# Second feed-forward layer as one block: expert tiles gather and send their own rows, the shared part on both sides of the expert loop

## The reference, cut to what matters

```python
xt = layernorm(x).reshape(-1, 256)                 # 2048 tokens
scores = softmax(xt @ gate_w.T)                    # 15 experts
topk_w, topk_idx = top_k(scores, 3)
topk_w = topk_w / (sum(topk_w) + 1e-20)
comb = zeros((T, 15)).at[arange(T)[:, None], topk_idx].add(topk_w)
h = einsum('td,efd->etf', xt, fc1_w) + fc1_b       # 512 wide per expert
a = gelu(h[..., 256:]) * h[..., :256] * geglu_mult
yexp = einsum('etf,edf->etd', a, fc2_w) + fc2_b
y = einsum('etd,te->td', yexp, comb)
hs = xt @ s_fc1_w.T + s_fc1_b                      # shared part, 2 x 512 wide
ys = (gelu(hs[..., 512:]) * hs[..., :512] * s_mult) @ s_fc2_w.T + s_fc2_b
x = x + y + ys
```

## Time and profile before

| | |
|---|---|
| time, median of 3 | 1479.79 us (1479.38 to 1481.75) |
| time of the profiled execution | 1479.18 us |
| its span | 1477.4 us |
| busy: TensorE, VectorE, ScalarE, GpSimd | 80%, 50%, 35%, 27% |
| mean granted TensorE clock | 0.863 |
| HBM traffic | 91 GB/s over the span |

### The profile page before, as it was taken

One profiled execution on the slowest core, in us unless ns is written; L12 is line 12 of the kernel. 1 busy time (PEld: TensorE's weight loads), 2 busy tenths in 40 slices (PEclk: granted clock), 3 DMA queues, 4 the chain that ended last, 5 costly groups with the idle time before them and its releaser, 6 DMA issues. The chain is left out here.

```text
span 1477.4 us, 20683 instructions
## 1 busy us (share of the span) xinstructions
PE 1175.2 (80%) x6778; PEld 768.4 (52%) x6779; DVE 732.5 (50%) x1364; ACT 521.5 (35%) x1084; POOL 399.5 (27%) x482
## 2 busy tenths in 40 slices
PE   4798993699999999944698989997539989999900
PEld 2323442699999999932243534443325455555500
DVE  5576622355665556453776676751421124444423
ACT  1285550344543345300265454644130112222200
POOL 3153456223332223023121120000066001111156
PEclk9698655799999999975699999979759999999955
DMA  3460101322333222034232231200853112222134
GB/s 97 171 264 23 51 27 43 109 93 72 112 122 112 82 70 81 19 111 128 72 112 91 73 102 52 66 1 1 261 184 142 54 47 82 82 82 78 64 103 132
DMA packets 86460, 135.49 MB, mean 92 GB/s; under 512 B 18504, under 2 KB 55468, under 8 KB 86258
## 3 DMA queue, kind: packets, MB, share of 16 engines
q1 hardware_dynamic: 72050, 92.58, 19.6%
q0 software_dynamic: 14336, 41.94, 8.2%
HBM read 86.98 MB, written 47.71 MB: 91 GB/s over the span
## 5 line engine op out<-in xcount | busy, mean ns | idle before, releaser
L1744 DVE TENSOR_REDUCE M<-S 128x2 f32<-128x1024 f32 x128 | 153.9, 1221 | 39.2 <-PE S L1389 35.1
L1651 ACT ACTIVATE PT<-S 128x512 f32<-128x512 f32 x256 | 138.8, 594 | 83.1 <-PE S L1413 81.3
L2110 PE MATMUL H<-W,XST 128*128 x248 | 122.1, 616 | 5.2 <-issue 5.1
L222 POOL TENSOR_TENSOR w12l<-stage,w12h 128x1024 fp32r<-128x1024 f32 x28 | 67.9, 2427 | 202.2 <-ACT w12h L216 202.1
L1197 DVE TENSOR_TENSOR HTm0l<-HFm,HTm0h 128x320 fp32r<-128x320 f32 x128 | 121.7, 951 | 1.0
L1203 DVE TENSOR_TENSOR HFm<-Um,SGm 128x320 f32<-128x320 f32 x128 | 62.4, 487 | 80.9 <-ACT SGm L1166 80.6
L1166 ACT ACTIVATE SGm<-Gm 128x320 f32<-128x320 f32 x128 | 55.9, 437 | 119.0 <-PE Um L1124 118.1
L2088 POOL DMA_DIRECT2D ys<-YS x62 | 33.5, 541 | 233.2 <-DVE YS L2204 233.2
L1137 PE MATMUL Ym<-w3h,HTm0h 128*128 128x256 f32 x320 | 93.3, 292 | 0.0
L909 DVE TENSOR_REDUCE M<-S 128x2 f32<-128x1024 f32 x64 | 77.1, 1222 | 30.4 <-PE S L426 29.9
L1389 PE MATMUL S<-KS,QS 48*128 48x512 f32 x256 | 70.3, 547 | 25.7 <-DVE M L1744 9.5
(11 more groups left out here) (273 smaller groups left out, 2485.0 us busy)
## 6 DMA issues: line engine op xcount, KB each, us to landing
stage<-in_W12T SPq DMA_DIRECT2D x32, 512.0 KB, 6.2
xs<-zeros POOLq DMA_DIRECT2D x25, 512.0 KB, 5.9
stage<-in_W3T SPq DMA_DIRECT2D x16, 512.0 KB, 3.8
XS<-xs SPq DMA_DIRECT2D x62, 128.0 KB, 2.0
ys<-YS POOLq DMA_DIRECT2D x62, 128.0 KB, 2.0
W<-in_fc1T SPq DMA_DIRECT2D x2, 3840.0 KB, 21.8
KS<-scrk SPq DMA_DIRECT2D x96, 64.0 KB, 2.3
QS<-scrq SPq DMA_DIRECT2D x96, 64.0 KB, 2.2
```

The source lines that it names most:

```text
L222: pool.tensor_tensor(ew.part(1, s, c), ew.stage[:, c % STAGES, :], ew.part(0, s, c).bitcast(F32), ALU.subtract).then_inc(ew.low_done, 1)
L1651: act.activation(PT[:, at % SLICES, 2 * hp + j, :], S2[:, j, :], ACT.Exp, scale=HP ** -0.5).then_inc(exp_done, 1)
L1744: dve.tensor_reduce(M[:, n % 3, at:at + 2 * TPB + 1:2 * TPB], out[:, :, :], AX.X, ALU.max).then_inc(S1.done(("max", c)), 1)
L2110: m = pe.matmul(H[:, c % 2, :], XST[:, c % 2, k, :], W1[:, k, bass.ds(e, 1), :], start=(k == 0), stop=(k == KD - 1))
```

## The change

`route1`, `experts1` and `combine` become one block, `ffn1`.

- The slot of every token-expert pair is no longer used to scatter rows. Instead a table says for each slot which pair sits in it: with lo and hi the low 7 bits and the rest of the slot's number, VectorE writes one-hots LO (128x1024) and HI (128x496) for 8 token tiles at a time, GpSimd multiplies HI by the pair's number + 1, and TensorE sums LO transposed by HV into a 128x62 table in PSUM. There are 6 such chunks. Empty slots get a target past the end.
- GpSimd gathers each expert tile's rows from XF in HBM (`fetch`) and scatters its 128 results to yk, ordered by pair (`send`, out-of-range targets are dropped). Fetch j+4 is written ahead of send j on GpSimd's queue. xs1 and its fills go.
- fc2_b is added to each expert tile's result on VectorE, in place of the product with comb; s_fc2_b is added to X by GpSimd.
- The shared part of batches 0 and 1 stays ahead of the expert loop, that of batches 2 and 3 follows it. There, the weighted addition of yk rows (loaded by SP, contiguous) is interleaved on VectorE with the shared part, one token tile after each of its elements.
- Layer 1 stores XF to HBM, and loads and scales the shared weights.

The diff, cut to its core:

```diff
 # layer0
-                (env.xs0, E0 * CAP0, filled0), (env.xs1, TILES1 * P, filled1)) for r in range(0, rows_, ZROWS)]
+                (env.xs0, E0 * CAP0, filled0),) for r in range(0, rows_, ZROWS)]
 # layer1
+                    if t == ends(b) + 6:
+                        sp.wait_ge(xn_done[1], b + 1)
+                        sp.dma_start(env.xf.rearrange("(b t p) d -> b p t d", p=P, t=TPB)[b],
+                                     XF[:, b % 2 * TPB:(b % 2 + 1) * TPB, :]).then_inc(env.xf_stored, 16)
+                if t == 40:
+                    load_shared()
+                if t == 90:
+                    pool.wait_ge(env.shared_loaded, 16 * 6)
+                    for j in range(FFS // P):
+                        ins_ = pool.tensor_scalar(env.s2[:, j, :], env.s2[:, j, :], smul[:, j:j + 1], None, ALU.mult)
 # ffn1, SP
+            for k in range(KF): W2 load
+            for k in range(KD): W1 load
+            sp.wait_ge(decoded, 1)
+            B1 load
+            sp.wait_ge(expert_done, 1)
+            B2 load
+            sp.wait_ge(h_ready, TILES1)
+            for c in range(DEEP):
+                sp.wait_ge(y_sent[c], LAST_YS[c])
+            for t in range(NT):
+                sp.dma_start(YK[:, t, :, :], env.yk.rearrange("(k t p) d -> t p k d", k=K1, p=P)[t]).then_inc(yk_loaded[t], 16)
+            for i, t in enumerate(finished):
+                sp.wait_ge(fin, i + 1)
+                out of tile t
 # ffn1, GpSimd
-                pool.dma_start(ys_tiles[j], YS[:, c, :]).then_inc(y_stored[c], 16)
+            def fetch(j):
+                if j >= DEEP:
+                    pool.wait_ge(xt_ready, j - DEEP + 1)
+                pool.indirect_dma_start(
+                    out=XS[:, j % DEEP, :], out_offset=None, in_=env.xf[:, :],
+                    in_offset=bass.IndirectOffsetOnAxis(ap=env.moves.source[:, j:j + 1], axis=0),
+                ).then_inc(fetched[j % DEEP], 16)
+            def send(j):
+                pool.wait_ge(y_done, j + 1)
+                pool.indirect_dma_start(
+                    out=env.yk[:, :], out_offset=bass.IndirectOffsetOnAxis(ap=env.moves.target[:, j:j + 1], axis=0),
+                    in_=YS[:, j % DEEP, :], in_offset=None, bounds_check=K1 * TOK - 1, oob_is_err=False,
+                ).then_inc(y_sent[j % DEEP], 16)
+            pool.wait_ge(decoded, 1)
+            for j in range(DEEP):
+                fetch(j)
+            for c in range(2, BATCH):
+                shared_bias(c)
+            for j in range(TILES1):
+                if j + DEEP < TILES1:
+                    fetch(j + DEEP)
+                send(j)
 # ffn1, TensorE
+            def place(i):
+                pe.wait_ge(hv_done, i + 1)
+                for t in range(TC):
+                    m = pe.matmul(table, LO[:, i % 2, t, :], HV[:, i % 2, t, :], start=(i == 0 and t == 0),
+                                  stop=(i == CHUNKS - 1 and t == TC - 1))
+                m.then_inc(hot_free, 1)
+            shared_in(0, 0), shared_in(0, 1), rank products, shared_in(0, 2), shared_in(0, 3)
+            place(0)
+            place(1)
+            for q in range(TPB):
+                shared_out(0, q)
+                place(2 + q)
+            shared part of batch 1; the 62 steps; shared part of batches 2 and 3
 # ffn1, VectorE
+            hot(0)
+            hot(1)
+            shared_gate(0, 2)
+            shared_gate(0, 3)
+            for q in range(TPB):
+                hot(2 + q)
+                shared_add(0, q)
+            table to target and source, tiles' experts, weights
-                dve.tensor_copy(YS[:, c % DEEP, :], Y[:, c % 2, 0:D]).then_inc(y_done, 1)
+                dve.tensor_tensor(YS[:, c % DEEP, :], Y[:, c % 2, 0:D], B2[:, bass.ds(e, 1), :].squeeze(1), ALU.add).then_inc(y_done, 1)
```

More of the change, by code:

```diff
@@ L1802, in _, with __init__, ffn1 @@
                         keep_logits(b)
-def combine(nc, env, ex, out):
+class Moves:
+    def __init__(self, sb):
+        self.val = sb("val1", [P, K1, NT])
+        self.source, self.target = sb("source1", [P, TILES1], U32), sb("target1", [P, TILES1], U32)
+FRONT = 2
+HALVES = 2
+CHUNKS = K1 * HALVES
+TC = NT // HALVES
+def ffn1(nc, env, ins, out):
+    JS, KF = FFS // P, FF1 // P
+    FIRST = TPB * FRONT
     with ExitStack() as ctx:
         sb, ps, sem = scope(nc, ctx)
[L1809 to L1829, removed]
@@ L1847, in route1 @@
[L1847 to L1855, removed]
@@ L1856, in route1 @@
[L1856 to L1891, removed]
@@ L2068, in steps @@
                 step(j // DEEP, j % DEEP)
-        xs_tiles = env.xs1[:, :].rearrange("(j p) d -> j p d", p=P)
-        ys_tiles = env.ys1[:, :].rearrange("(j p) d -> j p d", p=P)
+        back = [("in", c, j) if p == 0 else ("out", c, j) for c in range(FRONT, BATCH) for p, j in
+                [(0, j) for j in range(JS)] + [(1, q) for q in range(TPB)]]
+        each = -(-NT // len(back))
+        final, todo = [], list(range(NT))
+        for i, s in enumerate(back):
+            final.append(s)
+            if i >= 1:
+                final += [("rows", t) for t in todo[0:each]]
+                todo = todo[each:]
@@ L2073, in _ @@
+        final += [("rows", t) for t in todo]
+        finished = []
+        for i, s in enumerate(final):
+            for t in range(NT):
+                mine = [("rows", t)] + ([("out", *divmod(t, TPB))] if t >= FIRST else [])
+                if s in mine and all(m in final[0:i + 1] for m in mine):
+                    finished.append(t)
         @block.sync
         def _(sp):
-            def step(r, c):
-                j = r * DEEP + c
-                if not (isinstance(r, int) and j < DEEP):
-                    sp.wait_ge(xt_ready, j - DEEP + 1)
-                sp.dma_start(XS[:, c, :], xs_tiles[j]).then_inc(xs_loaded[c], 16)
@@ L2083, in _, with shared_bias @@
+            sp.wait_ge(sent, 16 * NT)
         @block.gpsimd
         def _(pool):
-            def step(r, c):
-                j = r * DEEP + c
-                pool.wait_ge(y_done, j + 1)
-                pool.dma_start(ys_tiles[j], YS[:, c, :]).then_inc(y_stored[c], 16)
-            steps(pool, step)
-            for c in range(DEEP):
-                pool.wait_ge(y_stored[c], 16 * ((TILES1 - c + DEEP - 1) // DEEP))
+            row = env.s2b[:, :].unsqueeze(1).to_broadcast([P, TPB, D])
+            def shared_bias(c):
+                xb = env.X[:, c * TPB:(c + 1) * TPB, :]
+                pool.tensor_tensor(xb, xb, row, ALU.add).then_inc(biased, 1)
@@ new lines, in shared_out @@
+            def shared_out(c, q):
+                t = c * TPB + q
+                pe.wait_ge(at_done, JS * (c + 1))
+                wait(pe, shared_done, t - 1)
+                for j in range(JS):
+                    m = pe.matmul(pw[:, t % 2, 0:D], AT[:, j, q * P:(q + 1) * P], s2[:, j, :],
+                                  start=(j == 0), stop=(j == JS - 1))
+                m.then_inc(ys_ready, 1)
+            def place(i):
[4 more added lines that the diff above has]
+                m.then_inc(hot_free, 1)
@@ new lines, in _ @@
+            shared_in(0, 0)
+            shared_in(0, 1)
+            pe.wait_ge(run_done, 1)
+            pe.matmul(rk[:, 0:NT, :], env.before[:, :], w.all[:, :, :], start=True, stop=False)
+            pe.matmul(rk[:, 0:NT, :], env.ones[:, :], w.run[:, 0:NT, :], start=False, stop=True)
+            pe.matmul(rk[:, NT, :], env.ones[:, :], w.run[:, NT, :], start=True, stop=True).then_inc(rk_ready, 1)
+            shared_in(0, 2)
+            shared_in(0, 3)
+            place(0)
+            place(1)
@@ L2180, in _ @@
             turn_back(*divmod(TILES1 - 1, DEEP))
+            act.wait_ge(a_done, TILES1)
+            for c in range(FRONT, BATCH):
+                for j in range(JS):
+                    gelu(c, j)
         @block.vector
         def _(dve):
-            dve.wait_ge(env.b1_loaded, 16)
+            link = Link(dve, chain)
+            pick(dve, link, env, w, E1, K1, env.lg[:, :, :], False)
+            dve.nop().then_inc(lg_sub, 1)
+            dve.wait_ge(ex_done, 1)
+            softmax_top(dve, link, env, w, E1, K1, 0.0)
@@ new lines, in _ @@
+            link(dve.tensor_tensor(sq[:, :, :], ntile[:, :].unsqueeze(1).to_broadcast([P, E1, E1]),
+                                   env.earlier[:, :, :], ALU.mult))
+            link(dve.tensor_reduce(base[:, :], sq[:, :, :], AX.X, ALU.add))
+            link(dve.scalar_tensor_tensor(
+                w.lg[:, :, :], base[:, :].unsqueeze(1).to_broadcast([P, NT, E1]), float(P), rk[:, 0:NT, :],
+                ALU.mult, ALU.add))
+            for k in range(K1):
+                link(dve.tensor_tensor(w.tmp[:, :, :], w.lg[:, :, :], w.hot[:, k, :, :], ALU.mult))
+                link(dve.tensor_reduce(w.slot[:, k, :], w.tmp[:, :, :], AX.X, ALU.add))
@@ new lines, in _ @@
+            link(dve.tensor_reduce(w.red[:, :], w.top[:, :, 0:K1], AX.X, ALU.add))
```

(27 more changed lines are left out.)

372 lines of the change are left out of this document (190 added, 182 removed).

## The result

The changed kernel took 1553.05 us (median of 4, 1546.12 to 1558.18) against 1480.77 us before: ratio 1.048, 95% interval 1.0428 to 1.0532. It is slower by 72 us; 43 us faster was forecast. The profiled execution has a span of 1554.6 us.

A forecast was written before the change was run, and what follows sets the result against it. Two TensorE-bound stages, then a result gather paced by GpSimd's indirect gathers with TensorE idle. Front -86, loop +62, tail -19 made -43: 1112.5 + 267.3 + 54.8 plus 1.8 gave 1436.4 us, range 1398 to 1466.

The forecast's parts named there:

- part 3: Start of the new block: first expert tile's transpose at about 1112.5 us against 1198.36, 86 us earlier.
- part 4: Expert loop: fetch behind send makes 4.38 us a tile instead of 3.30; +62 us, loop 267.3 us.
- so I keep it: Expert loop: despite gaps of 1 us in each step, the granted clock stays 1.00, the 2.4 GHz level.
- Rival C: Expert loop: gaps drop TensorE's clock to 1.2 GHz; loop 390 us, time about 1560 us; chance 0.05.
- Rival A: Expert loop: the fetch stays hidden, 3.3 us a tile; time 1374 us; chance 0.09.
- Rival B: Expert loop: fetch partly hidden or latencies cheaper, 3.7 to 4.0 us a tile; 1397 to 1415 us; chance 0.10.
- Rival D: Front stage: table latency, not TensorE, sets the pace; +15 to 25 us, 1451 to 1461 us; chance 0.10.
- part 5: Tail after the loop's last product: 54.8 us in place of 73.9 us, -19 in the sum.
- part 2: Layer 1: shared-weight loads at beat 40 stand ahead of group 4's shift rows; 1 us, ends 0 and 6.
- The skill's rule on the shared port: Expert loop: VectorE's gate and GpSimd excluding each other could add 0.43 us per two steps, 12 in all; none added.

The follow-up runs named there:

- filler3: The change plus three useless 128x256 products at the end of each TensorE step in the expert loop; 1511.3 us, ratio 1.0186 to the kernel before.
- before_pool: The kernel before, with the expert loop's plain load of tile j+4 issued by GpSimd ahead of the store of tile j; 1573.97 us, ratio 1.0583.
- ahead6: The change with fetch j+6 in place of fetch j+4 ahead of send j, same buffers; 1368.91 us, ratio 0.9228 to the kernel before.
- before_pool6: The kernel before, with plain loads issued by GpSimd, load j+6 ahead of store j; 1479.24 us, ratio 0.9972 to the kernel before.
- keep0: The change, adding expert 0's fc2_b row to every tile without the register read; 1566.03 us on a slower chip, ratio 1.0154 to the kernel before.
- biaslate: The change with fetch j+6 ahead of send j, and GpSimd's s_fc2_b additions moved behind its second and last table products; 1392.81 us on a slower chip.

## Why the prediction was wrong

- **Front (part 3): start of the loop right, 1112.87 for 1112.5, by terms that cancel.** A table chunk took 1.9 to 2.1 us at the full clock (3.4 at the slow one, once) where I chose 2.9 from a range of 1.8 to 4.0: 16 records of 62 columns cost hardly more than the slow row with 15 columns halved. TensorE still paced it, 3.6 us from one chunk to the next, and the table was 3.8 us shorter than forecast; batch 1 up to the first transpose took 22.4 us for 25.4. Against that, the first table product came at 1068.88 for 1061.7: VectorE's chain began with two operations that GpSimd's addition stretched by 3.8 us, and the attention ended 2.5 us later. B1, B2 and W2 were covered.
- **Loop (part 4): the step that failed.** The mechanism was named and right: the fetch behind the send, two steps to a cycle, TensorE waiting for XS. Two things in it failed: the sum of the cycle, 8.75 us forecast, 12.37 measured in the one shown and 12.8 on average; and the clock, which it kept at full speed. Term by term: from the step's start to the result on its way 7.44 for 4.40; of these 3.04 us, 1.64 are the slow H products, 0.63 a later start of H after a wait of TensorE, 0.6 the register read ahead of YS (the gap of 0.53 where they overlapped by 0.09), the rest unassigned. Hand-over to GpSimd 0.82 for 0.1, for which the forecast gave no row. The nearest one, the store behind YS in the same loop of the kernel before, starts 0.64 us after the result that is ready at 1304.52:

```profile
1305.16 0.54 POOL L2088 DMA_DIRECT2D ys<-YS  x1 [2.47 <-DVE YS L2204]
```

Queue 1.31 for 1.25. Landing 2.79 for 3.0 with the way to TensorE: the only one that was less. Of the 3.62 us, 1.64 are the clock's and 1.98 are not.
- **The clock: "so I keep it" was wrong.** It rested on one stretch of 5 us, 35% busy, between busy ones. The same trace, read a little wider around that stretch, shows a lower clock at a higher busy share (58%):

```profile
1015.00:1040.00 25.00, 14.53 (x96) 10.74 (x94) 5.70 (x17) 4.78 (x7) 1.20 (x2) 0.83 0.00 0
```

In the loop the gap comes again in every cycle. After a wait of 2.72 us H took 3.52; in filler3, after 0.88, it took 1.98. And before_pool speaks against the clock's holding even with the latencies as forecast: there, in the one trace, it fell in a cycle of 8.5 us. Rival C had the event, and by chance nearly the time (1560). Its reason, that a step's products alone take 6.3 us, did not come: TensorE was 70% busy and waited 101 us for rows. Nor was the clock needed for the sign: filler3 holds it at 0.97 and is slower than the kernel before by 1.9% all the same. Three latencies, the late start of H (0.63), the register read (0.6) and the hand-over (0.72 more), alone carried the cycle past the 5.1 us a tile at which the gain is eaten (5.33 in the cycle shown, 5.6 on average). C and the forecast were no alternatives: longer latencies make longer gaps, with them the clock falls, and this lengthens the cycle once more.
- **Rival A** (the fetch stays hidden, 1374 us) is what ahead6 is, 1369: without the order's cost the forecast's other terms come out. Rival B, cheaper latencies, did not come; they were dearer.
- **Rival D** did not come: TensorE paced the table.
- **Tail (part 5): right**, 53.1 us for 54.8; no wait for yk shows in it.
- **Layer 1 (part 2): right** in kind: the wait for shift rows came, 4.5 us in the changed kernel. What it cost the whole can't be told from 0.
- **The skill's rule on the shared port** I weighed at the wrong place. In the loop it changes nothing: the gate takes 0.429 us (0.426 before). At the block's start it holds. A copy of 240 elements took 2.47 us beside GpSimd's additions of 1024 (2.36 us for one) and 0.28 without, and an operation on two buffers 1.99 and 0.41. The Trainium skill ("SBUF — State Buffer", "SBUF: two separate sides") says that a GpSimd operation and an fp32 copy within SBUF on VectorE shut each other out for a whole instruction, and so do a GpSimd operation that reads SBUF and a VectorE operation with two SBUF inputs. At the block's start the traces agree; in the loop, with GpSimd's DMA instructions, they show none of it.

## What to carry to other kernels

When a load moves to a queue that also sends results, write the cycle down before anything else: from the use of the loaded tile to its result, through the send ahead in the queue, to the landing of the next load, divided by the number of steps it spans. If that is near the step's time, move the load up the queue; it needs no more buffers, as long as what it waits for comes before what the send waits for. And a gap in TensorE's work that comes back in each step must be priced at the slow clock too.

## What the runs showed of the hardware that I had not expected

- From the end of VectorE's result to the start of GpSimd's DMA instruction lie 0.82 us for the send (indirect) and 0.64 us for the store of the kernel before (plain), though GpSimd had waited for nothing else. In before_pool and before_pool6, where the stores are written out one by one in place of a loop, it is 0.29 us (in before_pool 1247.18 to 1247.47). That the loop makes the difference is not shown.
- In the changed kernel a register read of the tile's expert ahead of a VectorE operation leaves a gap of 0.4 to 0.55 us even when the value was known long before; without it the operation follows at once (keep0).
- After a wait for rows, H starts 1.06 us after the transpose of the next tile, where it starts 0.22 us after it in an unbroken flow (1306.10 to 1307.16, and 1311.60 to 1311.82). The profile puts the wait down to ScalarE's copy of that transpose, but by the program H of tile j needs only the copy of tile j, made a step earlier; between the two stands the read of the tile's expert on TensorE. Which it is was not tested.
- On one of the chips the kernel before took 1541.8 us in place of 1480 to 1485, with the same loop of 206 us in ahead6's variants. In those the extra time lies ahead of the new block, which starts at 1065.99 in biaslate and at 1037.09 in ahead6. For the kernel before it is open, and so is the cause; no profile of it was taken there.
